# Moving the first pair's scores ahead of the values, with a rearranged opening and flush

## The reference

```python
xn = ln(x, g_norm)
q = l2norm((xn @ Wq).reshape(b, n, 16, 64).transpose(0, 2, 1, 3)) * q_scale
k, v = split(xn @ Wkv)                     # one head of keys and values for all 16
k, v = concat([null_k, k]), concat([null_v, v])       # null key and value from cond_64
sim = einsum('bhid,bjd->bhij', l2norm(q), l2norm(k) * k_scale) * 8 + relative bias
attn = softmax(where(causal, neg, sim))    # bias of the null column: null_attn_bias
y = ln(einsum('bhij,bjd->bhid', attn, v) @ Wout, g_out)
xq = fake_quant(y)                         # one scale over the whole tensor
h = fake_quant(silu(xq @ Wg.T) * (xq @ Wu.T))
out = x + h @ Wd.T
```

## Time and profile before

| | us |
|---|---|
| median of three runs | 305.9 |
| the profiled execution's own time | 306.61 |
| its span, first to last instruction | 304.8 |
| busy: TensorE matmuls, VectorE, ScalarE, GpSimd | 256.9, 241.1, 227.8, 208.5 |
| opening and first rounds, to the values product of round 2 | 40.7 |
| four rounds in the middle of the loop, 120.78 to 150.06 | 29.28 |
| from the values product of round 32 to the end of the span | 47.4 |

### The profile page before, as it was taken

The page is one execution under the profiler, slowest core; times in us unless marked ns, Lnnn a source line. Parts: engine busy times, 40 slices in busy tenths (PEclk is TensorE's granted clock), DMA queues, the critical chain, the costliest instruction groups (busy, mean ns, idle before and its releaser), DMA issues.

```text
span 304.8 us, 7310 instructions
## 1 busy us (share of the span) xinstructions
PE 256.9 (84%) x2175; PEld 203.2 (67%) x2176; DVE 241.1 (79%) x967; ACT 227.8 (75%) x779; POOL 208.5 (68%) x394
## 2 busy tenths in 40 slices
PE   0649799999999999999999999999999988776260
PEld 0317678887778787878787877788787766561040
DVE  2978858898788788878887988788887776659993
ACT  1264858888888888888888888898888878249480
POOL 2789957887788778878887888778867764113301
PEclk9999899999999999999999999999999999999967
DMA  4269000000000000000000000000000020000013
GB/s 141 64 163 263 3 1 2 1 2 1 3 0 2 4 1 2 0 3 1 2 0 3 4 0 2 0 4 0 2 2 2 1 73 1 2 0 0 1 37 108
DMA packets 13083, 6.89 MB, mean 23 GB/s; under 512 B 1953, under 2 KB 12913, under 8 KB 13042
## 3 DMA queue, kind: packets, MB, share of 16 engines
q1 hardware_dynamic: 12466, 6.13, 7.5%
q10 hardware_dynamic: 576, 0.26, 0.4%
HBM read 5.31 MB, written 1.07 MB: 21 GB/s over the span
## 4 chain that ended last, share of the span: by engine, by line
PE 38%; ACT 18%; DVE 18%; issue 11%; POOL 7%; DMA 4%; SPq 1%; DVEq 0%; ACTq 0%; POOLq 0%
PE bank L843 10%; ACT prob L555 9%; PE front L826 5%; PE bank L800 5%; DVE score L1178 5%; DMA ks<-in_L_cond_k_scale_dram 4%; ACT pT L565 3%; PE back L886 3%; PE front L886 3%; PE back L826 3%; POOL rq L395 3%; POOL prob L442 2%; DVE hmax L1305 2%; DVE yn L1201 2%; DVE oT L1342 2%
## 5 line engine op out<-in xcount | busy, mean ns | idle before, releaser
L555 ACT ACTIVATE prob<-score,negmax 128x258 f32<-128x258 f32 (+1 forms) x256 | 113.4, 447 | 30.2 <-DVE negmax L1178 30.2
L442 POOL TENSOR_SCALAR prob<-prob,rrow 128x258 f32<-128x258 f32 x254 | 106.8, 438 | 29.0 <-DVE rrow L1186 26.0
L395 POOL TENSOR_TENSOR rq<-qn,neghalf 128x8 f32<-128x8 f32 x32 | 54.2, 1694 | 2.7
L843 PE MATMUL bank<-pT,val 128*64 128x256 f32 (+1 forms) x512 | 48.7, 332 | 5.6 <-ACT pT L565 3.9
L843 PEld LDWEIGHTS bank<-pT,val 128*64 128x64 f32 x512 | 31.7, 136 | 27.3 <-ACT pT L565 12.9
L555 ACT ACTIVATION_READ_ACCUMULATOR prob<-score,negmax 128x1 f32 x256 | 48.5, 190 | 0.0
L800 PE MATMUL bank<-wout,oT 128*128 128x128 f32 x256 | 36.8, 287 | 4.1 <-DVE yn L1201 2.3
L1039 DVE TENSOR_REDUCE qn<-sq 128x8 f32<-128x512 f32 x32 | 21.9, 684 | 22.8 <-ACT sq L512 22.3
L1178 DVE CUSTOM_DVE_ANT_0 score<-front,bias 128x258 f32<-128x258 f32 (+1 forms) x128 | 38.2, 354 | 1.6 <-PE front L826 1.0
L1178 DVE CUSTOM_DVE_ANT_0 score<-back,bias 128x258 f32<-128x258 f32 (+1 forms) x128 | 38.0, 353 | 0.4 <-PE back L826 0.4
L800 PEld LDWEIGHTS bank<-wout,oT 128*128 128x128 f32 x256 | 31.0, 191 | 8.5 <-issue 4.7
(11 more groups left out here) (197 smaller groups left out, 466.8 us busy)
## 6 DMA issues: line engine op xcount, KB each, us to landing
bias<-relative_table SPq DMA_DIRECT2D x8, 256.0 KB, 5.2
out_dram<-prob SPq DMA_DIRECT2D x4, 256.0 KB, 2.7
X<-in_x_dram SPq DMA_DIRECT2D x1, 896.0 KB, 12.3
prob<-in_L_cond_Wq_dram SPq DMA_DIRECT2D x1, 512.0 KB, 5.9
wout<-in_L_cond_Wout_dram SPq DMA_DIRECT2D x1, 512.0 KB, 13.5
prob<-in_L_ffn_w_down_dram SPq DMA_DIRECT2D x1, 176.0 KB, 2.4
X<-in_x_dram SPq DMA_DIRECT2D x1, 128.0 KB, 4.4
prob<-in_L_ffn_w_gate_dram SPq DMA_DIRECT2D x1, 128.0 KB, 2.4
```

The lines of the kernel that those rows point to most:

```text
L395: pool.tensor_tensor(dst, src, neghalf[:, 0:width], ALU.pow).then_inc(done, 1)
L442: pool.tensor_scalar(prob[:, par, h, cols], prob[:, par, h, cols], rrow[:, par, h, t:t + 1], 1.0, ALU.mult, ALU.mult).then_inc(normed, 1)
L555: act.activation(prob[:, par, h, cols], score[:, h % 4, cols], ACT.Exp, scale=-1.0, bias=negmax[:, par, h, t:t + 1], accum_out=rowsum[:, p ...
L843: last = pe.matmul(val_ps[a * D:a * D + D, pair * N + i0:pair * N + N], val[m % 2][:, blk, :], pT[:, 2 * pair + a, c0:c1], start=blk == 1, ...
```

## The change

Seven things change together.

1. In the rounds from 2 to 31 TensorE issues `first_scores`, `values`, `second_scores` in place of `values`, `scores` of pair 0, `scores` of pair 1. `first_scores` also waits for the first two copies of transposed probabilities of the round before. The program order of VectorE keeps `oT_copy` ahead of the first `score_pair`.
2. The null column of a sequence is transposed in one instruction in place of two, and only ahead of the fourth head's transposes; the row length `KEYS` grows so that both null columns of all heads lie at one stride. The null value's product gets 32 columns.
3. In the opening, three loads and the two loads of the null value go from SyncE's queue to ScalarE's, the mask row loses most of its memset on GpSimd and half of its work on VectorE, the bias net's second layer and the q quarters swap places on several engines, and the null value's columns are copied by ScalarE.
4. `null_output` goes ahead of the transposes of round 1, and two sets of `keep_busy` and the statistics of sequence 2 leave round 0.
5. The two rounds that drain the loop become `flush`, with the transposes of two heads ahead of `values`, the last values product in another bank, and the exponents of the last two heads spread between ScalarE's copies.
6. The maximum over the last sequence's y is taken straight from PSUM and scaled, and the scales of the feed-forward net are multiplied by GpSimd.
7. GpSimd's power for x moves by one round, and on VectorE `y_normalise` stands ahead of `invert`, and `k_norm2` behind `x_normalise`.

The diff, cut to what the text speaks of:

```diff
@@ -333,8 +336,6 @@
-            for dst, src in ((condk[:, :], row(cond[0])), (qs[:, :], row(q_scale)), (ks[:, :], row(k_scale))):
-                sp.dma_start(dst, src).then_inc(ld_keys, 16)
@@ -417,18 +418,18 @@
-            pool.memset(mrow[:, :, :], 0.0).then_inc(consts, 1)
-            pool.memset(ones_row[:, :], 0.0).then_inc(consts, 1)
+            pool.memset(mrow[:, :, 0:KEYS1 + 1:P + 1], 0.0).then_inc(consts, 1)
...
-            pool.memset(unull[:, :], 0.0).then_inc(null_zero, 1)
+            pool.memset(unull[:, :, :], 0.0).then_inc(null_zero, 1)
...
+            for q in range(2):
+                q_power(q, q)
...
-            for q in range(3):
-                q_power(q, q)
+            q_power(2, 2)
@@ -478,6 +482,10 @@
+            for dst, src in ((condk[:, :], row(cond[0])), (qs[:, :], row(q_scale)), (ks[:, :], row(k_scale))):
+                act.dma_start(dst, src).then_inc(ld_keys, 16)
+            for dst, src in ((vcol[0:D, :], col(cond[1])), (vcol[D:P, :], col(cond[1]))):
+                act.dma_start(dst, src).then_inc(ld_v, 16)
@@ -530,12 +540,17 @@
+            act.wait_ge(ld_mask, 16)
+            act.wait_ge(consts, 5)
+            keys1 = mrow[0:1, :, 0:KEYS1].rearrange("p b (t k) -> p b t k", t=2)[:, :, :, 1:P + 1]
+            mask_v = mask_u[:, :].rearrange("p (b n) -> p b n", b=B)[:, :, ::-1].rearrange("p b (t k) -> p b t k", t=2)
+            act.activation(keys1, mask_v, ACT.Copy, scale=-NEG, bias=NEG).then_inc(mask_ready, 1)
...
+            q_square(0, q_ps0[0])
...
-            q_square(0, q_ps0[0])
...
+            q_square(1, q_ps0[1])
...
-            q_square(1, q_ps0[1])
@@ -577,15 +598,19 @@
-                if s.turned is not None:
+                if s.turned is not None and s.live:
...
+                if s.g == 2 and s.next is not None:
+                    v_copy(s.next)
...
+                if s.at == GB * B - 1:
+                    exponent(heads(s.at)[2])
@@ -597,19 +622,22 @@
+                if s.at == GB * B - 1:
+                    exponent(heads(s.at)[3])
...
-                if s.g == 1 and s.next is not None:
-                    v_copy(s.next)
...
-                    act.copy(unull[0:H, :], misc[0:H, 0:C]).then_inc(unull_ready, 1)
+                    act.wait_ge(sel_ready, 1)
+                    for t in range(2):
+                        act.activation(unull[0:2 * H, t, :], misc[0:2 * H, 0:C], ACT.Copy,
+                                       scale=sel[0:2 * H, t:t + 1]).then_inc(unull_ready, 1)
...
-                    act.wait_ge(ld_misc, 16 * 5)
+                    act.wait_ge(ld_misc, 16 * 3)
@@ -730,12 +760,12 @@
-            pe.wait_ge(mask_ready, 1)
-            least = pe.value_load(mask_min[:, :])
+            q_make_first(1)
...
-            q_make_first(1)
+            pe.wait_ge(min_ready, 1)
+            least = pe.value_load(mask_min[:, :])
@@ -771,19 +801,18 @@
-                pe.wait_ge(kT_ready, 1)
-                pe.wait_ge(vnull_ready, 2)
+                pe.wait_ge(xT_ready, 4)
+                pe.wait_ge(vnull_ready, 4)
...
-                    last = pe.matmul(misc[0:H, 0:C], vnull[:, k, :], wout[:, k, :], start=k == 0, stop=k == HP - 1)
+                    last = pe.matmul(misc[0:2 * H, 0:C], vnull[:, k, :], wout[:, k, :], start=k == 0,
+                                     stop=k == HP - 1)
...
-            def null_weights(m, t):
...
-                at = KEYS1 if t == 0 else 0
-                product = pe.transpose(null_out(m)[:, t, :], prob[:, m % 2, :, at], ident[:, :])
-                if t == 1:
-                    product.then_inc(n_done, 1)
+            def null_weights(m):
...
+                pe.transpose(null_out(m), prob[:, m % 2, :, :].rearrange("p h k -> p (h k)")[:, ::KEYS1],
+                             ident[:, :]).then_inc(n_done, 1)
@@ -835,12 +864,14 @@
-                if at > 0:
+                last_group = at == GB * B - 1
+                ps = q_ps if last_group else val_ps
+                if at > 0 and not last_group:
...
-                            last = pe.matmul(val_ps[a * D:a * D + D, pair * N + i0:pair * N + N], val[m % 2][:, blk, :],
+                            last = pe.matmul(ps[a * D:a * D + D, pair * N + i0:pair * N + N], val[m % 2][:, blk, :],
@@ -872,40 +903,76 @@
+                else:
+                    pe.wait_ge(pT_ready, g - GH + 1)
...
-                if i >= 2 and s.null is not None and s.live:
-                    if i == 2:
-                        pe.wait_ge(normed, 2 * g + 4)
-                    null_weights(s.null, i - 2)
+                if i == 3 and s.null is not None and s.live:
+                    null_weights(s.null)
...
-            def group(s, masked):
-                if s.summed is not None:
-                    if s.g == 1 and s.prev is not None:
-                        pe.wait_ge(n_ready, s.prev + 1)
-                    values(s.summed)
+            def first_scores(s, masked):
...
-                if s.live:
-                    if s.g == 0:
-                        pe.wait_ge(kT_ready, s.b + 1)
-                        pe.wait_ge(qT_ready, 4 * s.b + 2)
-                    if s.g == 2:
-                        pe.wait_ge(qT_ready, 4 * s.b + 4)
-                    scores(s, 0, masked)
+                    pe.wait_ge(pT_ready, GH * (s.at - 2) + 2)
+                if s.g == 0:
+                    pe.wait_ge(kT_ready, s.b + 1)
+                    pe.wait_ge(qT_ready, 4 * s.b + 2)
+                if s.g == 2:
+                    pe.wait_ge(qT_ready, 4 * s.b + 4)
+                scores(s, 0, masked)
...
+            def second_scores(s, masked):
...
+                if s.g == 1 and s.prev is not None:
+                    pe.wait_ge(n_ready, s.prev + 1)
+                scores(s, 1, masked)
...
+            def flush():
...
+                s = Group(GB * B)
+                turn(s, 0)
+                turn(s, 1)
+                values(s.summed)
+                turn(s, 2)
+                turn(s, 3)
+                pe.wait_ge(yT_ready, B - 1)
+                null_weights(s.null)
+                for pair in range(2):
+                    y_products(s.summed, pair)
+                values(s.turned)
+                for pair in range(2):
+                    y_products(s.turned, pair)
+                y_null(s.null)
+                for k in range(3):
+                    w_turn(k)
+                down_scale_turn()
+                keep_busy(8, q_ps)
...
+            def group(s, masked):
+                if not s.live:
+                    return
+                if s.summed is not None:
+                    first_scores(s, masked)
+                    values(s.summed)
+                    second_scores(s, masked)
+                else:
+                    first_scores(s, masked)
...
-                    scores(s, 1, masked)
+                    second_scores(s, masked)
...
+                if s.at == 1:
+                    null_output()
@@ -916,32 +983,18 @@
-                if s.at == 0:
-                    keep_busy(6, bank[5])
...
-                if s.turned == GB * B - 1:
-                    pe.wait_ge(qT_ready, GB * B)
-                    for t in range(2):
-                        null_weights(s.null, t)
...
-                if s.first and s.g == 1:
-                    null_output()
-                if s.at == GB * B + 1:
-                    for k in range(3):
-                        w_turn(k)
-                    down_scale_turn()
-                    keep_busy(8, q_ps)
...
-                pe.wait_ge(f_v, 1 + 4 * k)
+                pe.wait_ge(f_v, 1 + 3 * k)
@@ -1096,14 +1158,6 @@
-            dve.wait_ge(consts, 7)
-            mask_v = mask_u[:, :].rearrange("p (b n) -> p b n", b=B)
-            dve.tensor_scalar(mrow[0:1, :, KEYS1 + 1:KEYS1 + P + 1], mask_v[:, :, ::-1][:, :, P:N], 1.0, -NEG,
-                              ALU.subtract, ALU.mult).then_inc(mask_ready, 1)
-            keys1 = mrow[0:1, :, 0:KEYS1].rearrange("p b (t k) -> p b t k", t=2)[:, :, :, 1:P + 1]
-            dve.tensor_scalar(keys1, mask_v[:, :, ::-1].rearrange("p b (t k) -> p b t k", t=2), 1.0, -NEG,
-                              ALU.subtract, ALU.mult).then_inc(mask_ready, 1)
-            dve.memset(ones_row[0:1, :], 1.0).then_inc(mask_ready, 1)
@@ -1114,13 +1168,13 @@
-            dve.wait_ge(ld_x, 16)
-            x_stats(1)
...
+            dve.wait_ge(ld_x, 16)
+            x_stats(1)
+            qT_evac(1, 1, 0)
...
-            qT_evac(1, 1, 0)
@@ -1227,14 +1274,15 @@
+                if s.turned == GB * B - 1:
+                    invert(heads(s.turned)[2:4])
+                    last_normalise()
...
-                if s.turned is not None:
-                    invert(heads(s.turned)[2:4])
-                if s.turned == GB * B - 1:
-                    last_normalise()
...
+                if s.turned is not None and s.live:
+                    invert(heads(s.turned)[2:4])
@@ -1243,23 +1291,24 @@
+                if s.at == 0:
```

(36 more changed lines are left out.)

74 lines of the change are left out of this document (44 added, 30 removed).

## The result

The changed kernel took 309.37 us, the median of four runs (308.69 to 309.89), against 305.45 for the kernel before in the same comparison: a ratio of 1.0118, interval 1.0076 to 1.0161. The profiled execution took 309.89 us with a span of 308.1, the one before 306.61 and 304.8.

The account below looks back on a forecast made before the run. VectorE's chain of scores was taken to pace TensorE in two rounds of four. Terms 7.4 - 3.1 - 0.7 = +3.6 us on 306.6 gave 310.2, or 309.5 against the median; it said 309.9, range 301.5 to 314.5.

Parts of the forecast that it names:

- The loop over S, q and v: S: VectorE's first score instruction starts; q: last q matmul ends; v: values product starts; new loop 7.40 us.
- S to q: From VectorE's first scores to the end of TensorE's last q matmul: 4.05 us, VectorE's chain pacing TensorE.
- Between q and v: On TensorE, the wait goes; first pair's scores, 0.65 us, and tile shape changes, 0.3 (ends 0 and 0.44), come in.
- The term of 0.2: Tile shape changes counted as 0.2 in place of 0.3 by the draining rule: 2.7 us less over 27 rounds.
- v to S: From the values product over VectorE's `oT_copy` to its first scores: falls only from 2.56 to 2.40 us.
- my 1.09: Loop's summed growth over four rounds, +1.09 us, 0.27 a round.
- The four kinds of rounds: Rounds from v to v: +0.59, +0.41 (with `y_normalise`), -0.14 (null column) and +0.23 us.
- The sum of the loop: Rounds 2 to 28, 27 rounds: +7.4 us, ends -0.7 and +11.
- The opening: Opening and first rounds: -3.1 us, ends -6 and -0.5; earlier scores, filled idle time and clock, 1.6 given back.
- Behind the loop: Flush and feed-forward: -0.7 us, ends -2 and +1; maximum from PSUM -0.3, GpSimd's product -0.2, last values about 0.2.
- What would show it: Trace signs: q to S 3.35, score waits every round, four rounds 30.4 us, busy share under 0.95; wrong under 29.3.
- my rivals: TensorE bound, 300.8 (0.17); switches free, 302 (0.08); half the loop growth, 306.5 (0.20); opening gives 0.5, 312.8 (0.10).

Follow-up runs that it names:

- e1: Kernel before with only the new TensorE order (first scores, values, second scores) in live rounds from 2 on; 312.64 us, ratio 1.0211.
- e4: Changed kernel with `y_normalise` ahead of `oT_copy` on VectorE; 304.69 us, ratio 0.9977.
- e7: Changed kernel with both pairs' scores ahead of the values product on TensorE; 328.17 us, ratio 1.0724.
- e8: e2 with GpSimd's power for x and VectorE's norm of k back in their old places; 297.98 us, ratio 0.9742.
- e2: Changed kernel with the order alone undone: values, first scores, second scores; 300.72 us, ratio 0.9837.
- after: The changed kernel with all its edits, against the kernel before; 309.37 us, ratio 1.0118.
- e3: Changed kernel with VectorE's first pair's scores ahead of its copy of the values product and the reciprocals; 308.33 us, ratio 1.0102.
- e6: Changed kernel with dummy transposes on TensorE in the flush, 8 and 10; 308.55 us, ratio 1.0103.
- e9: e8 with the edits of e4, e5 and e6 together; 297.24 us, ratio 0.9717.
- e12: e11 with e5's 2 and 8 dummy products of TensorE in the opening; 295.97 us, ratio 0.9659.
- e11: e8 with the loads of condk, qs and ks back on SyncE's queue; 296.57 us, ratio 0.9678.
- e5: Changed kernel with ten dummy transposes on TensorE in the opening, 2 and 8; 308.26 us, ratio 1.0070.

## Why the prediction was right, point by point

- **The loop over S, q and v.** Right. S to q was put at 4.05 and measures 4.03. e1 has the loop's whole loss, e4 takes 0.62 from its path and gains 0.64 a round, e7 adds 0.65 and loses 0.63.
- **Between q and v.** Put at 0.65 and 0.3, measured 0.95. The two changes of the tile shape are 0.09 and 0.21, where I took 0.1 and 0.2. The term of 0.2 that I drew from the rule was a misreading of mine: the loop is added up from q to v as a whole, so both changes belong in it, whatever the round had before. The Trainium skill (TensorEngine Tiling (Array Packing), Key Properties) says that a change of the tiling mode drains TensorE, and the trace does not speak against that: both changes cost time. In e8, in a round where nothing waits, q to the values takes 0.09 as well (123.44 to 123.53).
- **v to S.** Mis-sized: 2.26 where I said 2.40. The copy starts 1.57 after v as said, but from the copy to S it is 0.69 and not 0.83. I took the whole duration of the reciprocal, 0.18, which in the round of the earlier trace rows ended before a wait; followed at once by the next instruction, it holds VectorE for 0.09 (138.09 to 138.18). The other 0.05 is its start, 0.60 behind that of the copy where it had been 0.65. In four rounds the 0.14 is 0.56 of my 1.09.
- **The four kinds of rounds.** Put at 7.55, 7.40, 8.02, 7.40, measured 7.32, 7.53, 7.88, 7.24. Take 0.14 off each and three come within 0.1. The second is 0.27 above that, and its trace shows two parts:

```profile
120.51 1.52 PE L874 MATMUL bank<-pT,val 128*64 128x256 f32 x16
...
121.69 0.62 DVE L1083 SCALAR_TENSOR_TENSOR kz<-kv,rk,qks 128x128 f32<-128x128 f32 x2 [0.62 <-POOL rk L396]
122.24 0.68 DVE L1215 COPY oT<-bank 128x512 f32<-128x512 f32 x1
```

The copy starts 1.73 after v in place of 1.57, because `kz` waited 0.62 for k's power: 0.16, the moved power and norm of k, which I priced at nothing. I had named its cover, over 4 us of slack of GpSimd and ScalarE, but the norm is needed at once, and slack elsewhere in the round doesn't help. The rest is S to q, 4.16 here and not 4.03, and it is not the move's: e1, with the power and the norm in their old places, has 4.15 in this round, and its copy at 1.57. I had carried one S to q through all four kinds. With this order the move costs 0.16 a sequence (0.5 in the first), with the old one 0.47 (e2 against e8).
- **The sum of the loop.** +7.4 said, +5.64 measured, within the ends.
- **The opening.** -3.1 said, with round 2's values near 37.6; the profiled execution has 38.41, -2.34. From the first score to round 2's values it is 10.44 where it was 12.91, -2.47 against my -2.4; what is missing lies ahead of the first score. The seven profiled executions with this opening (after, e2, e3, e4, e6, e7, e8) have 36.18 to 38.41, mean 37.6. `null_output` in the idle time and the clock behind it came as said. The first score 0.7 earlier did not in this execution (27.97 against 27.84): the wait for `ks` gave way to one for `g1b`, and a q quarter ran at the lower clock.
- **Behind the loop.** -0.7 said, 0.0 measured. The part behind the last values product won 0.4, as counted. The new flush lost 0.4: it leaves TensorE idle for 0.81, 0.29 and 0.93 us, and the values product ran at the lower clock. Where it ran at the full clock, the sum against before is -1.3 in e6 and -1.1 in e4, which has the same flush without dummy products. So this execution met the lower clock and others did not.
- **What would show it.** q to S grew to 138.18 - 134.96 = 3.22 (said 3.35), and the idle time ahead of the copy by 0.6, as said. TensorE's wait for the scores ahead of the last transposes shows in 8 of 16 rounds and not in every one; in the other two kinds these transposes begin 0.07 and 0.14 behind the end of the scores with no idle time marked. TensorE also waits for the copy ahead of the output product, 4.5 us in 8 of the 16 rounds, which I had called free. The busy share under 0.95 did not show: it is 29.19 / 29.97 = 0.974. A pause for a change of shape counts as busy in these rows, so the share can't tell a stalled TensorE from a working one. The four rounds at 30.4 are 29.97, which is above the 29.3 at which I would have been wrong.

The number was right with a loop over-sized by 1.8 us against an opening and an end under-paid by 1.5 in this execution. The mechanism of the sign, that scores put ahead of the values are put into the loop, is shown; the close hit of the total is in part luck, since it needs these two errors to cancel. The last step of the sum was loose as well: it gave 309.5 against the median, and I said 309.9 without a term for the 0.4. The times of my rivals were counted from the profiled execution's 306.6, so they stand 0.7 too high beside a median.

## What to carry to other kernels

When work is moved ahead of another on a busy engine, find the loop that sets the round, mark where it enters and leaves that engine, and ask if the moved work now lies between these marks; the idle time that it fills may be the cheaper of the two. Undo such a change piece by piece: here the order cost 8.6 us (6.9 when put alone into the kernel before) and hid that the rest of the change was worth 5.0, and with two small moves undone as well 7.9 (e8). An idle time that an engine has in every round is the place for work off the loop, as `y_normalise` showed, but only while that work's own input has come by then; in e9 it had not, and held back what stands behind it.

## What the hardware showed that I had not expected

- The same opening met the lower clock (0.50 of full speed, 1.2 GHz) in some executions and not in others. From 20.00 to 22.80 us the granted clock was 0.50, 0.53, 0.50 and 0.50 in the traces of after, e2, e6 and e8, and 1.00 in those of e3, e4 and e7. The first score came at 27.66 to 28.75 in the former and at 25.97 to 26.85 in the latter. The flush does the same: in e12, e11 with dummy products in the opening alone, the values product of round 32 took 2.43 us, in e11 1.52. The three traces with dummy products in the opening (e5, e9, e12) and the two with them in the flush (e6, e9) all have the full clock there, which speaks for them but is too few to show it. So a difference of 1 or 2 us in one trace's opening says nothing about an edit, and the runs of one kernel spread by as much or more (e3 307.19 to 310.7).
- The busy time of TensorE contains the pauses around tile shapes. After and e8 issue 253 matmul records each in four rounds, and are busy for 29.19 and 28.17 us: one change more in each round, up to 0.25 apiece. e7 has no such change more and is busy for 28.53, so 0.09 of the 0.25 a round can come without one; what it is I have not found.
